# Swapping the two arms of a branch on TensorE, and moving two weight blocks' load and split earlier, in a one-core graph-network and mixer kernel

## The reference, cut to what matters

```python
xn = _layernorm(x, axis=-1)
deg = segment_sum(ones, dst, n)
inv_deg = where(deg > 0, 1 / maximum(deg, 1), 0)[:, None]
def sage_conv(h, W_l, b_l, W_r):
    aggr = segment_sum(h[src], dst, n) * inv_deg
    return aggr @ W_l + b_l + h @ W_r
# each expert: two layers of relu(sage_conv(...)), the two best of a gate are summed
x = x + gnn(xn) + mixer(xn[None])[0]
x = x + ffn(_layernorm(x))       # a small bit-shift unit
```

## Time and profile before

| | |
|---|---|
| median of 3 runs | 1995.31 us (1994.72 to 1996.55) |
| the profiled execution | 1996.55 us |
| its span, first to last instruction | 1994.7 us |
| TensorE busy with matmuls | 1817.4 us (91%), 9484 of them |
| VectorE, ScalarE, GpSimd busy | 863.6, 646.3, 617.9 us |
| mean granted TensorE clock | 0.975 of full speed |

### The profile page before, as it was taken

One profiled execution on the slowest core, in us unless ns is written; L12 is line 12 of the kernel. 1 busy time (PEld: TensorE's weight loads), 2 busy tenths in 40 slices (PEclk: granted clock), 3 DMA queues, 4 the chain that ended last, 5 costly groups with the idle time before them and its releaser, 6 DMA issues. The chain is left out here.

```text
span 1994.7 us, 26833 instructions
## 1 busy us (share of the span) xinstructions
PE 1817.4 (91%) x9484; PEld 1500.0 (75%) x9484; DVE 863.6 (43%) x1776; ACT 646.3 (32%) x1210; POOL 617.9 (31%) x507
## 2 busy tenths in 40 slices
PE   1798999999999999959999889999989998899993
PEld 1455788888888787847789877887777988688883
DVE  8996311111111146545565456222566554552236
ACT  7843311111111211015536523211265455222210
POOL 4004432423231333115321107433361210154422
PEclk9999999999999999989999999999999999999997
DMA  2165812213121566235702000111175020011102
GB/s 62 41 151 122 82 64 95 79 73 122 53 100 42 218 225 184 90 112 125 230 29 89 27 1 25 40 43 36 46 198 158 27 95 22 1 43 43 54 26 67
DMA packets 112020, 166.45 MB, mean 83 GB/s; under 512 B 42683, under 2 KB 60842, under 8 KB 110898
## 3 DMA queue, kind: packets, MB, share of 16 engines
q1 hardware_dynamic: 111913, 165.05, 28.7%
HBM read 103.24 MB, written 55.53 MB: 80 GB/s over the span
## 5 line engine op out<-in xcount | busy, mean ns | idle before, releaser
L778 PE MATMUL ps<-yT,wslot 128*128 128x500 f32 (+1 forms) x576 | 208.3, 362 | 7.9 <-ACT qpT L1790 4.7
L779 PE MATMUL ps<-yT,wslot 128*128 128x500 f32 (+1 forms) x576 | 206.8, 359 | 0.0
L780 PE MATMUL ps<-yT,wslot 128*128 128x500 f32 (+1 forms) x576 | 206.6, 359 | 0.0
L1021 PE MATMUL ps<-g,adj 125*128 125x512 f32 (+1 forms) x800 | 186.3, 395 | 1.9 <-DVEq L1156 1.2
L2141 POOL TENSOR_TENSOR wslot<-mix_landing,wslot 128x512 fp32r<-128x512 f32 x96 | 126.9, 1352 | 185.2 <-ACT wslot L1727 185.2
L1021 PEld LDWEIGHTS ps<-g,adj 125*128 125x128 f32 (+1 forms) x800 | 150.2, 188 | 38.0 <-DVEq L1156 1.6
L2146 POOL TENSOR_TENSOR hidT<-qpT,hidT 128x500 fp32r<-128x500 f32 (+1 forms) x96 | 103.2, 1079 | 212.6 <-DVE hidT L1931 212.6
L1790 ACT ACTIVATE qpT<-ps,all_cols 128x500 f32<-128x500 f32 (+1 forms) x96 | 58.1, 610 | 312.7 <-PE ps L780 266.7
L778 PE MATMUL ps<-parts,w 128*128 128x500 f32 (+1 forms) x384 | 136.1, 354 | 2.2 <-PEq L559 2.2
L779 PE MATMUL ps<-parts,w 128*128 128x500 f32 (+1 forms) x384 | 136.0, 354 | 0.0
L780 PE MATMUL ps<-parts,w 128*128 128x500 f32 (+1 forms) x384 | 136.0, 354 | 0.0
(11 more groups left out here) (291 smaller groups left out, 3687.0 us busy)
## 6 DMA issues: line engine op xcount, KB each, us to landing
mix_landing<-in_L_mix_W SPq DMA_DIRECT2D x16, 1024.0 KB, 5.1
qk_dram<-qk_parts SPq DMA_DIRECT2D x128, 125.0 KB, 2.4
g_dram<-staged SPq DMA_DIRECT2D x40, 256.0 KB, 2.0
u_dram<-staged SPq DMA_DIRECT2D x40, 256.0 KB, 2.0
g_in<-g_dram SPq DMA_DIRECT2D x40, 256.0 KB, 3.8
u_in<-u_dram SPq DMA_DIRECT2D x40, 256.0 KB, 2.7
k_stack<-qk_dram SPq DMA_DIRECT2D x8, 1250.0 KB
q_stack<-qk_dram SPq DMA_DIRECT2D x8, 1250.0 KB
```

The source lines that it names most:

```text
L778: nc.tensor.matmul(out, lhs_high, rhs_high, start=first, stop=False)
L779: nc.tensor.matmul(out, lhs_high, rhs_low, start=False, stop=False)
L780: return nc.tensor.matmul(out, lhs_low, rhs_high, start=False, stop=last)
L1021: last = nc.tensor.matmul(m.ps[0:counts.shape[1], t % 2, :], counts if exact else counts.bitcast(F32), part if exact else part.bitcast(F32 ...
```

## The change

Four things are edited. The load of the two weight blocks no longer waits for the degree sums. ScalarE makes the high halves of both blocks before the first mean, not around sums 4 and 5. VectorE makes their low halves just before and just after the mean of sum 3. And at both branches on `top_sum` the condition is turned round and the arms are swapped: the arm for large counts stands first now, and the arm that runs with small counts is the `Else` arm.

```diff
-        WEIGHTS_FROM = (NC3 + 1, NC3 + 2)
...
                 emit_counts_out(m, sp, adj_dram, NG - 1)
-                sp.wait_ge(deg_summed, NC3)
                 for n, W in enumerate((Wl, Wr)):
                     sp.dma_start(m.landing[:, n], ...).then_inc(m.landed[n], 16)
...
-                with pe.If(top_sum <= EXACT_COUNTS):
+                with pe.If(top_sum > EXACT_COUNTS):
+                    sums(False)
+                with pe.Else():
                     sums(True)
-                with pe.Else():
-                    sums(False)
...
-                def weight_high(n):
+                act.wait_ge(xn_low, K)
+                for n in range(2):
                     act.wait_ge(m.landed[n], 16)
                     nc.scalar.activation(m.w1[:, n, 0], m.landing[:, n], ACT.Copy).then_inc(m.w_high, 1)
-                act.wait_ge(xn_low, K)
                 for n, (f, (c0, cn)) in enumerate(SUMS):
-                    if n in WEIGHTS_FROM:
-                        weight_high(WEIGHTS_FROM.index(n))
...
+                weight_low(0)
                 mean_of(NC3)
+                weight_low(1)
                 vec.wait_ge(small_summed, INV_TURNED)
...
                     mean_of(n)
-                    if n in WEIGHTS_FROM:
-                        weight_low(WEIGHTS_FROM.index(n))
...
-                with pe.If(top_sum <= EXACT_COUNTS):
+                with pe.If(top_sum > EXACT_COUNTS):
+                    all_counts_times_g(False)
+                with pe.Else():
                     all_counts_times_g(True)
-                with pe.Else():
-                    all_counts_times_g(False)
```

## The result

The changed kernel took 2003.60 us (median of 16 executions, 1997.29 to 2012.81) against 1993.05 for the kernel before in 16 executions (1985.41 to 1997.94). The ratio is 1.0055, with a 95% interval of 1.0043 to 1.0067: about 11 us slower (8.6 to 13.4). The forecast was slower by 4.2 us, with 2003.0 as the upper end of its range. The kernel before came out 2.3 us lower in 16 executions than in the three that the forecast started from, so the forecast time was missed by 4.1 us and the forecast difference by more, 6 to 7 us.

What follows compares the result with a forecast made beforehand. TensorE was taken to bound the kernel, so only its waits count. The terms, 4.2 (entry 3.68 + collision 0.5) + 0 + 0 + 0 = 4.2 us, took the median from 1995.31 to 1999.5 us, range 1996.8 to 2003.0.

Steps and rivals of the forecast that it cites:

- rival E: Behind the first branch's jump: the fetched page ends soon, next fetch outlasts the first matmuls; 1 to 2 us more, chance 0.07.
- What bounds the kernel: TensorE, busy 91% of the span; no waits inside the sums, and a delayed start of the first sum delays everything behind.
- Entry, the jump by itself: First branch: the entry becomes the far jump with nothing ahead to hide it; 3.68 us, or 3.25 by the other row.
- What the jump collides with: First branch: its instruction packet meets the last counts and early weight loads on DMA; 0.5 us added.
- The bound of 2.8 us: First branch: upper bound on the collision, the packet waiting behind one whole weight block, from landing times 8.2 - 5.4.
- the quiet price: First branch, as a rival: early loads do not touch the fetch, entry costs 3.25 to 3.68 us; chance 0.28.
- Clock: Before the degree sums: clock already 0.50, so longer idle time finds it there and the same climb follows; cost 0.
- Exit and second branch: First arm's exit gains at most perhaps 0.1 us; second branch's far jump lies under TensorE's 1.2 us wait, cost 0.
- Weights on their own: Early load, ScalarE's roundings and VectorE's subtractions around the sums: cost 0 on TensorE's path, gain 0.
- The range: Whole kernel: 1996.8 us, if the jump is partly quicker than any row, to 2003.0.
- rival B: Second branch's jump exposed: 0.4 to 2.3 us plus 1.7 of clock on top of 4.2; 2001.6 to 2003.5, chance 0.11.

Runs made afterwards that it cites:

- e1: Both branches swapped, weight loads and splits as before, against the kernel before: ratio 1.0016 (1.0003 to 1.0028), 1993.15 against 1991.16 us.
- e8: The changed kernel with both weight loads waiting for the first degree sum: ratio 1.0019 (1.0009 to 1.0029).
- e3: Only the first branch swapped, against the kernel before: ratio 1.0019 (1.0007 to 1.0031).
- quiet runs: Runs with the first branch swapped and no weight load ahead of its jump: e1, e3 and e8; ratios 1.0016, 1.0019 and 1.0019.
- padding runs: The changed kernel with 32 or 1 dead matmuls ending the arm not run; experts' first matmul 5.8 or 10.8 us later than before.
- e7: The changed kernel with only the first weight block loaded at once; one execution, jump 6.40 us, experts' first matmul 6.2 us later than before.
- e4: Only the second branch swapped, against the kernel before: ratio 0.9992 (0.9980 to 1.0004).
- e2: Only the weight blocks' load, roundings and subtractions moved, both branches as before, against the kernel before: ratio 1.0000 (0.9987 to 1.0013).
- e5: The changed kernel with 32 dead matmuls at the end of the arm not run: ratio 1.0021 (1.0012 to 1.0030).
- e12: Kernel before with early weights and unread matmuls at the end of counting (12) and behind the transposes (8): ratio 0.9972 (0.9953 to 0.9992).

## Why the prediction was wrong

Two terms failed, both on the path from the first branch to the sums. The collision of the jump with the early loads was put at 0.5 us and measured 2.8. The fetch of the next page was put at nothing in the sum, and at 1 to 2 us as rival E; it measured 5.5, 2.8 idle and 2.7 at half clock. The first alone would have left the time inside the range.

**What bounds the kernel: right.** TensorE waits for no mean and no weight block inside the sums; what delays their start is passed on in full (11.6 us at the experts, 11.8 at the counts times g).

**Entry, the jump by itself: right.** 3.25 to 3.68 us were forecast from the two exits; with no load ahead of it it measured 3.37, 3.68 and 3.94 in e1, e8 and e3, the last a little above.

**What the jump collides with: the term that was mis-sized.** I took 0.5 us, the difference in a packet's own duration, and kept 2.8 us as a bound. Measured were 6.19 less 3.77, 2.4 us by the row I had used, and 2.2 to 2.8 by the quiet runs (2.8 against e1, whose idle time before the degree sums was 5.30 us and not 8.12). The packet's own duration is no measure of it: the time is spent before the packet starts, behind the first block, which was issued 0.8 us before the branch. The bound of 2.8 us, taken from the landing times, had the right mechanism, and I gave it no weight in the sum. That it also fits to a tenth is luck: it is the gap between two landings, not what was left of the first block when the packet was due.

**Rival E, the second page: its mechanism came true, at a chance of 0.07 and with too low a price.** I let the next fetch take 3 us, at the quiet price, and so covered by a dozen matmuls. Queued behind the second block and the first stores it came late: 2.8 us idle. The padding runs speak for a page's end; e1, e7 and e8, with the same code on TensorE, show no gap when the packet comes promptly (between 179.0 and 179.5 us in e8, right behind its jump).

**Clock: wrong with two idle times.** "A longer idle time finds it at the lower level already" holds for the first. I did not see that a second one, after 4 us of work at 0.50, would be followed by 5.4 us more at 0.50: 2.7 us.

**Exit and second branch: right.** The gap at the stage's end stayed 2.2 us and the one before the counts times g 1.2 us; e4 is the same as before.

**Weights on their own: right.** e2 is 1.0000. ScalarE's two roundings began at 191.7 us and the low halves on VectorE at 209.4 and 212.5, the second drawn out to 4.8 us beside GpSimd; no matmul waited for either. What I missed is that a load can be free for its engines and dear for the instruction stream: alone 0, ahead of a far jump 8 us.

**The range.** Its upper end was named as that of rival B and put at 2003.0, while B's own sum ends at 2003.5; the measured 2003.60 lies above both. B itself did not happen.

The sum by the measured terms: 3.3 (jump, 5.30 less 1.96) + 2.8 (behind the block, 8.12 less 5.30) + 2.8 (second page) + 2.7 (second stretch at half clock) = 11.6, where I had 3.7 + 0.5.

By the Trainium skill's two-page rule (Runtime: NRT & Kernel Launch, Instruction fetch mechanics) a far jump fetches its target's page before it goes on; the changed kernel agrees with it, with one packet of q8 inside the 6.19 us. e5 shows that where the target lies matters behind the jump too.

## What to carry to other kernels

Put the arm that runs right behind its compare: a far jump is free only where the engine has queued work or waits for another anyway. Look at what is queued on DMA in the microsecond before a jump; a bulk load of 1 MB just ahead of it delayed the fetch by 2.8 us here, and the load behind it the next page too. A second idle time soon after a first can cost as much again in clock: here 2.8 us idle brought 2.7 us of half clock with it. That one idle time of the same total would have been cheaper is argued, not run.

## What the runs showed of the hardware that was not expected

- An instruction packet waits behind a 1 MB load that was issued 0.8 us before the branch (jump 6.19 us; 6.40 with a single block) and not behind two of which the first was issued 0.3 us after it (3.84 us).
- One matmul that never runs, placed ahead of the arm, moved a stall of 2.8 us inside it; 32 of them removed it, and with it 5.8 us (experts +5.8 against +11.6).
- The clock stays at 1.00 over this stage's start when matmuls on constants fill the idle time, and the sums then end 1.5 us earlier, counted from the end of counting (e12).
